# Four chunks of edges to a transfer instead of one or two, in a four-layer graph network on one Trainium2 core

## What is computed

```python
def _genconv(h, edge_attr, src, dst, w1, b1, g1, bb1, w2, b2, t):
    msg = relu(h[src] + edge_attr) + 1e-7
    m = msg * t
    seg_max = segment_max(m, dst, num_segments=3125)
    ex = exp(m - seg_max[dst])
    denom = segment_sum(ex, dst, num_segments=3125)
    alpha = ex / (denom[dst] + 1e-16)
    agg = segment_sum(msg * alpha, dst, num_segments=3125)
    z = relu(layernorm((h + agg) @ w1 + b1, g1, bb1))
    return z @ w2 + b2
e = edge_attr @ enc_edge_w + enc_edge_b                  # the same in all layers
h = genconv(h, e, ...)                                   # layer 0
for i in 1..3:  h = h + genconv(relu(layernorm(h)), e, ...)
```

## Time and profile before

| | |
|---|---|
| median of 3 runs | 4319.33 us (4317.49 to 4326.74) |
| the profiled execution | 4317.04 us |
| its span, first to last instruction | 4315.2 us |
| mean granted TensorE clock | 0.678 |
| busy: PE, DVE, ACT, POOL | 57%, 67%, 41%, 71% of the span |
| DMA traffic | 307125 packets, 469.66 MB, mean 109 GB/s |

### The profile page before, as it was taken

How to read it: one execution, slowest core, us unless ns; L and a number is a source line. 1 busy time by engine, 2 the same in 40 slices (tenths; PEclk the granted TensorE clock), 3 DMA queues, 4 the chain that set the end, 5 groups by cost and what they waited for, 6 DMA issues and landing times.

```text
span 4315.2 us, 37180 instructions
## 1 busy us (share of the span) xinstructions
PE 2470.6 (57%) x9731; PEld 1778.7 (41%) x9731; DVE 2874.9 (67%) x3973; ACT 1759.0 (41%) x3487; POOL 3058.1 (71%) x3248
## 2 busy tenths in 40 slices
PE   4666776665555555555555555555555555555554
PEld 3555555543433333333433333333343333333333
DVE  5888888875566666666656666666664666666665
ACT  2444444444433443334334433444343334443344
POOL 3777777775577777777557777777746777777773
PEclk9776667666566666666557666666656667666765
DMA  3545554554233333333223333333323333333332
GB/s 86 148 142 146 148 142 142 147 146 139 65 105 105 109 104 104 105 105 109 77 72 109 105 101 108 105 109 105 101 70 87 102 108 105 109 105 101 108 105 64
DMA packets 307125, 469.66 MB, mean 109 GB/s; under 512 B 169424, under 2 KB 175306, under 8 KB 306893
## 3 DMA queue, kind: packets, MB, share of 16 engines
q1 hardware_dynamic: 200286, 356.83, 24.0%
q0 software_dynamic: 103552, 109.52, 12.6%
q10 hardware_dynamic: 3054, 0.71, 0.1%
HBM read 217.93 MB, written 248.86 MB: 108 GB/s over the span
## 4 chain that ended last, share of the span: by engine, by line
POOL 69%; issue 23%; PE 2%; DVE 2%; DMA 1%; ACT 1%; POOLq 0%; ACTq 0%; DVEq 0%; SPq 0%
POOL zsrc L521 68%; POOL node_sw L532 1%; DMA zsrc<-z_rows,idx_all 1%; PE pT L801 0%; PE pR L898 0%; PE pX L790 0%; DMA node_sw<-sw_rows,row_idx 0%; PE pX L723 0%; PE pX L879 0%; DVE z L1295 0%; DMA sw_rows<-sw_out 0%; ACT sq L654 0%; ACT sw_out L614 0%; POOLq L517 0%; DMA z_rows<-z 0%
## 5 line engine op out<-in xcount | busy, mean ns | idle before, releaser
L521 POOL DMA_INDIRECT zsrc<-z_rows,idx_all x3136 | 2960.4, 944 | 1089.2 <-issue 979.3
L790 PE MATMUL pX<-ident,zsrc 128*128 128x128 f32 x2368 | 591.8, 429 | 1207.0 <-DMA zsrc<-z_rows,idx_all 1206.8
L614 ACT ACTIVATE sw_out<-pT 128x512 f32<-128x512 f32 x784 | 425.3, 594 | 1822.9 <-PE pT L801 1821.2
L790 PEld LDWEIGHTS pX<-ident,zsrc 128*128 128x128 f32 x2368 | 505.6, 316 | 1521.6 <-DMA zsrc<-z_rows,idx_all 1521.6
L1117 DVE TENSOR_TENSOR_SCAN S<-decay,S,pX 128x512 f32<-128x512 f32 x296 | 378.1, 1277 | 691.2 <-ACT decay L606 688.5
L801 PE MATMUL pT<-ident,S 128*128 128x128 f32 x1568 | 630.4, 406 | 46.2 <-DVE W L1121 46.2
L801 PE MATMUL pT<-ident,W 128*128 128x128 f32 x1568 | 619.3, 400 | 0.0
L1100 DVE TENSOR_TENSOR_SCAN M<-pR,M,u 128x512 f32<-128x512 f32 x296 | 376.8, 1273 | 235.1 <-ACT u L601 235.1
L785 PE MATMUL pX<-attr_pair,edge_w 128*128 128x512 f32 x592 | 435.4, 825 | 12.6 <-ACT attr_pair L593 12.5
L790 PE MATMUL pA<-ident,zsrc 128*128 128x128 f32 x768 | 195.0, 434 | 426.8 <-DMA zsrc<-z_rows,idx_all 426.8
L599 ACT ACTIVATE r<-pX,edge_b 128x512 f32<-128x512 f32 x296 | 204.7, 692 | 494.8 <-PE pX L790 494.8
(11 more groups left out here) (201 smaller groups left out, 3130.9 us busy)
## 6 DMA issues: line engine op xcount, KB each, us to landing
sw_rows<-sw_out SPq DMA_DIRECT2D x392, 512.0 KB, 2.9
attr_pair<-attr_cols SPq DMA_DIRECT2D x153, 512.0 KB, 4.6
zsrc<-z_rows,idx_all POOLq DMA_INDIRECT x3136
attr_in<-in_edge_attr_dram SPq DMA_DIRECT2D x196, 128.0 KB
attr_cols<-attr_pair SPq DMA_DIRECT2D x49, 512.0 KB, 3.1
max_cols<-M SPq DMA_DIRECT2D x49, 256.0 KB, 3.1
z_rows<-z SPq DMA_DIRECT2D x25, 125.0 KB
node_sw<-sw_rows,row_idx POOLq DMA_INDIRECT x100, 2.5
```

The costliest lines, as they stand in the source:

```text
L521: pool.indirect_dma_start(zsrc[c % RING][:, t4, h, :], None, z_rows, bass.IndirectOffsetOnAxis(idx_all[:, h, t4, c:c + 1].bitcast(U32), 0) ...
L614: act.activation(sw_out[c % 2][:, :, 2 * b:2 * b + 2, :, :].rearrange("p h t s c -> p (t s) h c"), pT[b][:, :].rearrange("p (a h c) -> p a ...
L790: last = pe.matmul(messages_bank(c, first_layer)[:, t4:CH:SUB], zsrc[c % RING][:, t4, :, :].rearrange("p h c -> p (h c)"), ident[:, :], st ...
```

## The change

Four chunks form a "four" (FOUR = 4); there are NF = 25 of them, the last one with two chunks (96 and 97).

- **Sums.** `sw_out` has room for four chunks, in two buffers. SP stores a four in one DMA of 2 MB, 16 KB per partition (`store_sw`), when its last chunk's copy is there. The sums of the last four are stored chunk by chunk (`store_sw_chunk`, 4 KB per partition into rows that lie 16 KB apart). In DRAM a partition's rows of four chunks lie side by side, so the row numbers that DVE computes change (`rows_of_edges`). The unused half of the last four is written once, in layer 0 after chunk 93, from what lies in the buffer, 1 MB.
- **Attributes.** Three buffers of four chunks (`attr_four`, ARING = 3) take the place of seven of two. A store or a load moves 1 MB, 8 KB per partition. In the layers 1 to 3 the loop loads fours 3 to 24 (`next_layer`); fours 0 to 2 are loaded in `end_layer`, behind the two small loads for the seam, in every layer, the last one too.
- **Maxima.** `M` holds four chunks, in two buffers; in layer 0 one DMA stores four chunks' maxima, 1 MB, 8 KB on each of 64 partitions.
- **Counters.** The numbers that are waited for follow (`SW_STORES`, `A_USES`); a copy of sums waits for its buffer once per four.
- Some tiles that are used once share room with others (`drops`, `dst_d`, `rank_cols`, `src_cols`, `sq1`, `sq2`), since the new buffers take more.

```diff
-EMPTY_ROW = 2 * HALF
+EMPTY_ROW = 25 * 4 * 2 * CH
...
-NPAIR = NCH // 2
-PRING = 7
+FOUR = 4
+NF = (NCH + FOUR - 1) // FOUR
+FOURS = [range(f * FOUR, min((f + 1) * FOUR, NCH)) for f in range(NF)]
+ARING = 3
+SW_STORES = [len(range(s, NF - 1, 2)) + (len(FOURS[-1]) if (NF - 1) % 2 == s else 0) for s in range(2)]
...
-        attr_pair = [sb(f"attr_pair{b}", [P, 2 * CH]) for b in range(PRING)]
+        attr_four = [sb(f"attr_four{b}", [P, FOUR * CH]) for b in range(ARING)]
-        M = two("M", [P, 2 * CH + 1])
+        M = two("M", [P, FOUR * CH + 1])
-        sw_out = two("sw_out", [P, 2, SUB, 2, H])
+        sw_out = two("sw_out", [P, FOUR, 2, SUB, 2, H])
...
+            def store_sw(g0, f):
+                sp.wait_ge(back_sb, 2 * g0 + 2 * (FOURS[f][-1] + 1 + PRE))
+                sp.dma_start(sw_four[f, :, :, :].rearrange("p q x -> p (q x)"),
+                             sw_out[f % 2][:, :, :, :, :, :].rearrange("p q h t s c -> p (q h t s c)")).then_inc(sw_stored[f % 2], 16)
...
-                    if c % 2:
-                        q = c // 2
+                    f = c // FOUR
+                    if c == FOURS[f][-1]:
                         sp.wait_ge(attr_sb, c + 1)
-                        sp.dma_start(attr_cols[q, :, :], attr_pair[q % PRING][:, :]).then_inc(cols_stored[q % PRING], 16)
-                    elif c >= 2:
-                        store_m(0, c // 2 - 1)
-                    if c >= 2:
-                        store_sw(0, c - 2)
-                for q in range(PAHEAD):
-                    sp.wait_ge(cols_stored[q], 16 * PUSES)
-                    sp.wait_ge(x_mm, done(2 * (NPAIR - PRING + q) + 1))
-                    load_cols(q)
+                        n = len(FOURS[f]) * CH
+                        sp.dma_start(attr_cols[f, :, 0:n], attr_four[f % ARING][:, 0:n]).then_inc(cols_stored[f % ARING], 16)
+                    if c % FOUR == 1 and f >= 1:
+                        store_m(0, f - 1)
+                        store_sw(0, f - 1)
+                        if f == NF - 2:
+                            unused = slice(len(FOURS[-1]), FOUR)
+                            sp.dma_start(sw_four[NF - 1, :, unused, :].rearrange("p q x -> p (q x)"),
+                                         sw_out[(NF - 1) % 2][:, unused, :, :, :, :].rearrange("p q h t s c -> p (q h t s c)")).then_inc(zero_stored, 16)
...
             def next_layer(g0):
-                for c in range(NCH):
-                    if c % 2 == 0:
-                        sp.wait_ge(x_mm, done(g0 + (c - 1)))
-                        load_cols((c // 2 + PAHEAD) % NPAIR)
-                    if c >= 2:
-                        store_sw(g0, c - 2)
+                for f in range(1, NF):
+                    if f + ARING - 1 < NF:
+                        sp.wait_ge(x_mm, done(g0 + FOURS[f - 1][-1]))
+                        load_cols(f + ARING - 1)
+                    store_sw(g0, f - 1)
...
+                if first_layer_end:
+                    store_m(g0, NF - 1)
+                for c in FOURS[-1]:
+                    store_sw_chunk(g0, c)
...
                 sp.dma_start(seam_sw1[:, :], seam_row_ap).then_inc(seam_in, 16)
+                for f in range(ARING):
+                    if first_layer_end:
+                        sp.wait_ge(cols_stored[f], 16 * A_USES[f])
+                    load_cols(f)
...
                 for s in range(2):
-                    pool.wait_ge(sw_stored[s], l * (8 * NCH) + 8 * (NCH + 2))
+                    pool.wait_ge(sw_stored[s], l * (16 * SW_STORES[s]) + 16 * (SW_STORES[s] + 1))
...
+                def rows_of_edges(row, j, part):
+                    first = j
+                    for n, times in ((SUB, 2 * SUB * FOUR - SUB), (CH, 2 * SUB - 2 * CH * FOUR), (CH * FOUR, 2 * CH * FOUR - 2 * SUB * FOUR)):
+                        whole(part, j, n, times)
+                        v.tensor_tensor(row, part, first, ALU.add)
+                        dve.drain()
+                        first = row
```

## The result

| | before | after |
|---|---|---|
| median of 20 runs | 4318.35 us (4317.06 to 4326.74) | 4325.18 us (4324.22 to 4333.94) |
| ratio, 95% interval | | 1.0016 (1.001 to 1.0022) |
| profiled execution | 4317.04 us | 4333.94 us |
| its span | 4315.2 us | 4332.1 us |

The change costs 6.8 us, 0.16%: inside the forecast range and within what I had called no change, and on the slow side of it with an interval that excludes 1. The twenty runs agree so well that the loss is clear of noise.

The account below looks back on a forecast made before the run. POOL's stream of gathers was taken to bound the kernel, so only tails and node stages could show the change. 4317.04 + 0 + 0 + 3.2 (node stages) + 0.6 (counter) = 4320.8, forecast as 4321 us, range 4312 to 4332.

Parts of the forecast that it names:

- The stream: POOL's chunk loop: 3136 gathers at 944 ns plus 0.31 us of issue stay untouched; cost 0.
- rival C: Chunk loop: gathers starve behind large descriptors, PE lagging over 29 us; hundreds of us, from 4400 up; chance 0.02.
- the new row numbers: DVE at chunk 85: 18 more small steps, 4.0 us, covered by idle time and PE's 29 us; cost 0.
- The tail of layer 0: Layer 0's last gather meets 3.5 MB instead of 4 MB: between -3.9 and +3 us, 0 taken.
- The burst in the chunk loop: Layer 0, each fourth chunk: maxima and sums together, 8.4 us, hidden since PE may start 29 us late; cost 0.
- Packets in turn: Layer 0's last gather: engines take queues in turn, making it 1.3 us late instead of 3.9, the sum 2.6 lower.
- Rival A: Six loads leave layer 0's tail, packets take turns, the node stage absorbs all: 4314 us; chance 0.14.
- The node stage: 3 MB of attribute loads beside the first node gathers delay `aggregate(0)`: 0 to 3.7 us, 0.8 taken per stage, +3.2.
- Rival B: Node stage: 3 MB hold seam and first gathers, delay passes whole, over 2.0 us per stage: 4332 us; chance 0.12.
- The counter: POOL's second semaphore number before the first node gather: 0 to 0.77 us, 0.15 taken four times, +0.6.

Follow-up runs that it names:

- all three edits: Changed kernel with the node stage's loads late, layer 0's chunk 97 burst held back and the clearings of M behind the indices: 4311.01 us, ratio 0.9983.

## Why the prediction was right, and where it was off

**The stream: right.** 3136 gathers at 944 ns with 0.31 of issue in both, POOL's wait for PE under 5 us, rival C off the table. PE's start behind a chunk's last gather reached some 11 us at most, at chunk 88 of layer 0, where 29 would have been needed:

```profile
947.99 0.94 POOL L543 DMA_INDIRECT zsrc<-z_rows,idx_all  x1 [0.30 <-issue]
...
958.90 1.57 PE L816 MATMUL pX<-ident,zsrc 128*128 128x128 f32 x8
```

That lag comes with the new row numbers. The small VectorE steps ahead of it take 11.2 us against 6.1 before, 5.1 more where 4.0 were taken, and in both kernels with 4 KB pieces, which do without 12 of the steps, PE starts 5.8 to 5.9 us behind the gathers of that chunk. It cost nothing, as forecast.

**The tail of layer 0: the mechanism right, the size wrong.** I took 0 between -3.9 and +3, arguing that 3.5 MB are nearly as much as 4 MB. The 3.5 had the maxima twice as large as they are; it was 3.0 MB, 8.4 us at 375 GB/s and not 9.8. (The burst in the chunk loop was 2.5 MB, 7.0 us and not 8.4, which changes nothing under the 29.) So by bytes the tail should have gained, and the upper end, worked out the same way, would have been about +1.6. Measured: +1.7 in the tail, PE 8.6 instead of 6.3 to 6.7 us late. So the measured value stands at that end, and the room that the stated +3 left above it came from the slip, which is luck. Bytes alone were the wrong measure. Before, most of the 4 MB was issued behind the last gather (six loads, spread over 3.7 us from 1035.50 on the earlier trace rows); after, all 3.0 MB stood ahead of it. That the place ahead makes the difference is my reading and no run separates it. Piece size is the second part, and is shown: 4 KB pieces take 1.5 us off. With the burst gone the same gather lands in time for a start at 2.45 us, so the whole cost is 6.1 us, of which the kernel before already paid some 4.

**Packets in turn: the price that I gave it is refuted, the rule is not.** I took each turn as one packet of the profile, that is one piece. So priced, this gather would be 1.3 us late behind pieces of 16 KB; it was 6.1, and 4.6 with 4 KB pieces, where that price gives 0.3. The Trainium skill (DMA: Bandwidth & Descriptors, Queues, rings and completion order) says that an engine drains a whole packet, typically about 9 to 17 descriptors, from one ring before it switches to another. No run here shows how many pieces make up such a packet, so the rule itself is neither borne out nor refuted. Rival A needed PE at 2.4 us behind the last gather and a node stage that absorbs all; neither came.

**The node stage: right.** 0.8 us per stage was taken, +3.2; two profiles give +3.8, and moving the loads gives 3.1 back. `aggregate(0)` was 2.7 to 3.4 us late in the four layers, near the upper end of 3.7, and the waits behind it absorbed most of it, as followed: in the layers 0 to 2 the last store of node rows was issued 0.8 us later (56.45 after the first node gather on the mean, against 55.63). Rival B needed 2.0.

**The counter: no sign of it.** 0.6 was taken; the three later tails are 0.5 us shorter in all, which is scatter. It was near the lower end, 0.

**The start: left out of the sum.** The sum looked at the DMAs, the waits and the new arithmetic, and costed the copies into `M` at nothing, but not the clearing of a buffer that had become twice as wide. It stands on the path to the first gather, and moving it moved that gather. 2.0 us, as much as the tail. With it and the tail's 1.7 the sum would have been 4317.0 + 2.0 + 1.7 + 3.2 = 4323.9 (without the counter's 0.6) in place of 4320.8, against the 4323.7 + 1.8 = 4325.5 of the second profile's execution.

Two small errors (0 for 1.7, nothing for 2.0) thus stood on the same side, and the range held because its upper end had been set by rival B, which did not happen. That is luck too. Of the 6.9 us the 3.8 of the node stages were forecast for the reason that the runs show; the 2.0 of the start and the 1.7 of the tail were not in the sum, and the rest, -0.6, is scatter.

## What to carry to other kernels

Where one engine's stream sets the time, ask of each larger transfer only whether it can be in flight beside a stage's last gather, or its first; one wait that holds it back for 7 us gave 6 of the 7 us back here. Do not judge it by bytes: 3.0 MB, in larger pieces and ahead of the gather, cost more than 4 MB around it. A buffer that grows is also cleared, and the clearing counts wherever it stands ahead of the first instruction of the bounding engine. And look for the same fault in the kernel before: moving its own six loads gave 3 us.

## What I had not expected of the hardware

A gather that meets a full queue can be held back altogether, not just slowed. In the first profile of the kernel before, between 1037 and 1041 us, SP's queue took 97.1% of the engines and POOL's queue all but nothing: 16 packets with 0.00 MB, where a gather has 32; the last gather's 32 packets, issued at 1035.75, then went within one microsecond, at 1041, while SP's queue was still as busy as before and stayed so for five more.

DMA of the kernel before from 1037 to 1041 us (queue, packets, MB, share of 16 engines), then from 1041 to 1042:

```profile
q1 hardware_dynamic: 358, 1.34, 97.1%
q0 software_dynamic: 16, 0.00, 0.3%
```
```profile
q1 hardware_dynamic: 111, 0.39, 95.3%
q0 software_dynamic: 32, 0.03, 9.3%
```

The second profile of the same kernel has two such steps, one gather at 1039 to 1040 and the last at 1041 to 1042. POOL's queue from 1037 to 1039, then 1039 to 1040, then 1041 to 1042:

```profile
q0 software_dynamic: 2, 0.00, 0.5%
q0 software_dynamic: 28, 0.03, 13.3%
q0 software_dynamic: 31, 0.03, 9.2%
```

In the second profile of the changed kernel, 1038 to 1044 us, the packets trickle: 63 in 6 us, as many as two gathers have.

```profile
q1 hardware_dynamic: 160, 2.04, 97.1%
q0 software_dynamic: 63, 0.08, 3.5%
```

What an engine holds ahead of the gather, a count of descriptors or of bytes, is not settled: the run with 4 KB pieces shows that both the size of a piece and something beyond it matter. The other open point is the 1.4 us that 4 KB pieces gave outside the tail of layer 0, in the profile in the node stages, where no store of sums is in flight any more. With all three edits single profiles have 244.3 us with 4 KB pieces against 246.0, but that rests on one stage, layer 0's (58.9 against 61.2, where two other profiles with the loads late have 59.6 and 59.7); the other three sum to 185.4 against 184.8, and the medians differ by 0.8 us.
